# One b2 product for both experts of a tile: class-wise b2 rows and a third register a tile in a GNN + top-2 MoE kernel

## The chip, the cores and the metric

The kernel runs on one core of a Trainium2 chip. The metric is the device time of one execution in microseconds. Three executions of the kernel before took 361.08, 362.18 and 362.03 us, median 362.03.

## What is computed

```python
# x: (64 graphs, 128 nodes, 128), adj: (64, 128, 128), f32 / int32
def gnn(h, adj, W, a):                       # graph attention
    Wh = h @ W
    e = leaky_relu(s1[:, :, None] + s2[:, None, :], 0.2)    # s1, s2 = Wh @ a1, Wh @ a2
    attn = softmax(where(adj > 0, e, -9e15), axis=2)
    return attn @ Wh
def ffn(x, gate_w, gate_b, W1, b1, W2, b2):  # 8 experts, D = 128, H = 256, top 2
    probs = softmax(xf @ gate_w + gate_b)
    top2_vals, top2_idx = top_k(probs, 2)    # weights cw[token, expert], not renormalised
    for each expert e: acc += cw[:, e] * (gelu(xf @ W1[e] + b1[e]) @ W2[e] + b2[e])
x = x + gnn(layernorm(x), adj, W, a)
x = x + ffn(layernorm(x), ...)
```

There are 64 x 128 = 8192 tokens, and each goes through two of eight experts.

## The kernel before, in words

The program has two parts. The first works on groups of 8 graphs (8 groups): layer norm, attention, the first residual, and the router. The router gives every token an unordered pair of experts, one of NC = 28 classes, and a place in the region of its class; POOL scatters the rows of each graph to `sorted_rows` in HBM by these places. Part two runs over NT = 91 tiles of 128 rows, each of one class, so that a tile needs just two experts.

Which rows and which experts a tile has is known only at run time. It stands in a table, `tile_rows`, with three numbers a tile: its first row, its first expert, its second expert. DVE works it out in the last group in small steps (`early_1` to `early_10`; `of_tile` has one row for each of the three numbers), TensorE turns the columns into rows with one product for each number (`turn_table`, L1339), and ACT copies them into `tile_rows` (`copy_table`, L524), where every engine reads them. A second table, for the tiles from NE = 21 on, is made in the same way (`late_1` to `late_12`) between the first eleven tiles and turned at tile 11.

In the loop over tiles, SP loads the rows `xt` (with a register load for the first row), ACT normalises them into `xn` (L557), TensorE transposes (`turn`, L1354), ACT copies to `xnT` (L538), DVE copies W1 and b1 of the two experts to `pair_w` (L846, a register load for each expert), TensorE makes the four products upward (`up`, L1364), ACT applies gelu and writes `hid` (L548), TensorE makes the products downward (`down`, L1383 and L1385), DVE adds the two experts' results, weighted, to the residual (L1170, L1173), and POOL scatters the rows to `out`.

TensorE's order of one tile n is: load a register with the first expert (L1369); `turn(n + 2)`; `up(n + 1)`; load the second expert's register; `down(n)`. `down` has for each expert k one bf16 product that opens the accumulation, a stationary 65 x 128 of ones with b2's row as the moving operand (65 partitions, because b2 is split in three bf16 parts on partitions 0, 32 and 64), and two f32 products with W2. b2's parts lie in the last 128 columns of each expert's block in `experts`, as the upper halves of f32 words, and are therefore read with a step of 2. In program order the waits of `turn` (L1353), `up` (L1360) and `down` (L1378) stand between them as semaphore instructions.

b2's three parts are made by POOL at the start in eight steps, counted by `b2_step` (L357 to L372); TensorE waits for the eighth only at tile 0. After it POOL has nothing to do until the first rows are scattered at 69 us.

Of the kernel before, what the change touches and what calls it, by code (L numbers as in the profile page):

```python
# [7 lines left out]
BF16 = mybir.dt.bfloat16  # L8
I32 = mybir.dt.int32
ALU = mybir.AluOpType  # L10
ACT = mybir.ActivationFunctionType
AX_X = mybir.AxisListType.X

P = 128
GB = 8
E = 8
HC = 2
NC = E * (E - 1) // 2
# [7 lines left out]
SHIFT, RSTD, CWA, CWB, TOK = 128, 129, 130, 131, 132  # L26
B1 = HC * P
W2C = B1 + HC
B2C = W2C + HC * P
WCOLS = B2C + P  # L30
XR = 12
WR = 3
NO_TOKEN = 1 << 20
# [2 lines left out]
XB = 5  # L36
WB = 3
BOUNDED = "the table holds numbers of experts, 0 to 7"
EPS = 1e-5


def build(nc, x, adj, W, a, gate_w, gate_b, W1, b1, W2, b2, out, sorted_rows):
# [7 lines left out]
    with ExitStack() as ctx:  # L50
        def sb(name, shape, dt=F32):
            return ctx.enter_context(nc.sbuf_tensor(name, shape, dt))

        def sem(name):
            return ctx.enter_context(nc.semaphore(name))

        wh_ps = ctx.enter_context(nc.psum_tensor("wh_ps", [P, 3, 512], F32))
        at_ps = ctx.enter_context(nc.psum_tensor("at_ps", [P, 3, 512], F32))
# [6 lines left out]
        ones_bf = sb("ones_bf", [P, 512], BF16)  # L65
# [6 lines left out]
        class_no = sb("class_no", [P, NC])  # L72
# [3 lines left out]
        pair = sb("pair", [P, 2, NC])  # L76
# [14 lines left out]
        b2_raw = sb("b2_raw", [65, E, P])  # L91
        b2_part = sb("b2_part", [65, E, P], BF16)
        b2_rest = sb("b2_rest", [65, E, P])
        experts = sb("experts", [P, E, WCOLS])
        pair_w = sb("pair_w", [P, WR, 2, W2C])

# [41 lines left out]
        tiles_i = sb("tiles_i", [P, NC], I32)  # L138
        cum = sb("cum", [P, 2, NC])
        here = sb("here", [P, 3, NC])  # L140
        of_tile = sb("of_tile", [P, 3, NC])
        early_rows = sb("early_rows", [P, NC])
        clip = sb("clip", [P, 2, NC])
        tile_cols = sb("tile_cols", [P, 2, 3])
        tile_rows = sb("tile_rows", [1, 2, 3, P], I32)


        xt = sb("xt", [P, XR, ROW])
# [18 lines left out]
        b2_step = sem("b2_step")  # L167
# [35 lines left out]
        early_step = sem("early_step")  # L203
        table_step = sem("table_step")
# [91 lines left out]
        def _(pool):  # L296
# [30 lines left out]
            for hi in range(2, E + 1):  # L327
                at = (hi - 1) * (hi - 2) // 2
# [25 lines left out]
                rstd_of_start(g)  # L354


            nc.gpsimd.memset(experts[:, :, B2C:WCOLS], 0.0).then_inc(b2_step, 1)  # L357
            pool.wait_ge(b2_loaded, 48)
            pool.wait_ge(b2_step, 1)
            nc.gpsimd.tensor_copy(b2_part[:, :, :], b2_raw[:, :, :]).then_inc(b2_step, 1)  # L360
            pool.wait_ge(b2_step, 2)
            nc.gpsimd.tensor_copy(experts[0:1, :, B2C:WCOLS], b2_part[0:1, :, :]).then_inc(b2_step, 1)
            pool.wait_ge(b2_step, 3)
            nc.gpsimd.tensor_tensor(b2_rest[:, :, :], b2_raw[:, :, :], b2_part[:, :, :], ALU.subtract).then_inc(b2_step, 1)
            pool.wait_ge(b2_step, 4)
            nc.gpsimd.tensor_copy(b2_part[:, :, :], b2_rest[:, :, :]).then_inc(b2_step, 1)
            pool.wait_ge(b2_step, 5)
            nc.gpsimd.tensor_copy(experts[32:33, :, B2C:WCOLS], b2_part[32:33, :, :]).then_inc(b2_step, 1)
            pool.wait_ge(b2_step, 6)
            nc.gpsimd.tensor_tensor(b2_raw[:, :, :], b2_rest[:, :, :], b2_part[:, :, :], ALU.subtract).then_inc(b2_step, 1)  # L370
            pool.wait_ge(b2_step, 7)
            nc.gpsimd.tensor_copy(experts[64:65, :, B2C:WCOLS], b2_raw[64:65, :, :]).then_inc(b2_step, 1)  # L372
            pool.wait_ge(b2_step, 8)

            for g in range(NG - 1):
                pool.wait_ge(place_step, PL * (g + 1))
# [3 lines left out]
            last = (NG - 1) * GB  # L380
# [8 lines left out]
        def _(act):  # L389
# [131 lines left out]
            def copy_table(late):  # L521
                src = at_ps if late else wh_ps
                act.wait_ge(table_done, late + 1)
                nc.scalar.activation(tile_rows[0:1, late, :, :].rearrange("o k n -> o (k n)"), src[0:1, 2, 0:3 * P], ACT.Copy)\  # L524
                    .then_inc(table_ready, 1)

            copy_rank(NG - 2)
            copy_table(0)
            rough_rstd(NG - 1)
            exp_router(NG - 1)  # L530
# [43 lines left out]
        def _(dve):  # L574
            def stats_at_start(g):
# [4 lines left out]
                if g >= 1:  # L580
# [95 lines left out]
            def norms_2(i):  # L676
# [43 lines left out]
            m1, k1, total, p1, e2, p2, k2, df, qa, qb, hi, lo, tri, cls = (small[:, j, :] for j in range(14))  # L720
# [143 lines left out]
            def early_4():  # L864
                dve.wait_ge(early_step, 3)
                nc.vector.tensor_copy(cum[:, 0, :], tiles_i[:, :])
                nc.vector.tensor_copy(here[:, 2, :], tiles_i[:, :])
                nc.vector.tensor_scalar(part[:, :], part[:, :], float(P), None, ALU.mult)
                nc.vector.tensor_copy(of_tile[:, 1:3, :], pair[:, :, :]).then_inc(early_step, 1)

            def early_sum(k):
                step = 1 << k
# [21 lines left out]

            def early_8():
                dve.wait_ge(early_step, 12)
                nc.vector.tensor_tensor(of_tile[:, :, :], of_tile[:, :, :], here[:, None, 2, :].broadcast_to([P, 3, NC]),
                                        ALU.mult).then_inc(early_step, 1)

            def early_9():  # L900
# [218 lines left out]
            def late_5():  # L1119
                dve.wait_ge(table_step, 4)  # L1120
                nc.vector.tensor_copy(cum[:, 0, :], tiles_i[:, :])
                nc.vector.tensor_copy(here[:, 2, :], tiles_i[:, :])
                nc.vector.tensor_copy(of_tile[:, 1:3, :], pair[:, :, :]).then_inc(table_step, 1)

            def late_sum(k):
                step = 1 << k
# [18 lines left out]

            def late_9():
                dve.wait_ge(table_step, 13)
                nc.vector.tensor_tensor(of_tile[:, :, :], of_tile[:, :, :], here[:, None, 2, :].broadcast_to([P, 3, NC]),
                                        ALU.mult).then_inc(table_step, 1)

            def late_10():
# [53 lines left out]
        def _(pe):  # L1205
# [126 lines left out]
            def turn_table(late):  # L1332
                dst = at_ps if late else wh_ps
                if late:
                    pe.wait_ge(table_step, 17)
                else:
                    pe.wait_ge(early_step, 15)
                for k in range(3):
                    last = nc.tensor.matmul(dst[0:1, 2, k * P:(k + 1) * P], tile_cols[:, late, k:k + 1], ident[:, :],  # L1339
                                            start=True, stop=True)  # L1340
                last.then_inc(table_done, 1)
# [2 lines left out]
            turn_table(0)  # L1344
            keep_busy_later(16)
            count_ranks(NG - 1)

            experts_bf = experts[:, :, :].bitcast(BF16)

            def turn(n):  # L1350
                pe.wait_ge(xn_ready, n + 1)
# [16 lines left out]
            def load_expert(n, k):  # L1368
                return nc.values_load(entry(n, 1 + k), engines=[mybir.EngineType.PE], min_val=0, max_val=E - 1,  # L1369
                                      skip_runtime_bounds_check_because=BOUNDED)  # L1370

            def down(n, chosen_pair):
                pe.wait_ge(hid_ready, n + 1)
                if n == 0:
                    pe.wait_ge(b2_step, 8)
                    pe.wait_ge(experts_loaded, 48)
                if n >= 2:
                    pe.wait_ge(o_step, OS * (n - 1))  # L1378
                for k in range(2):
                    cols = slice(k * P, (k + 1) * P)  # L1380
                    e = chosen_pair[k]
                    b2_rows = experts_bf[0:65, bass.ds(e, 1), 2 * B2C + 1:2 * WCOLS:2]
                    nc.tensor.matmul(at_ps[:, n % 2, cols], ones_bf[0:65, 0:P], b2_rows, start=True, stop=False)  # L1383
                    for c in range(HC):
                        last = nc.tensor.matmul(at_ps[:, n % 2, cols], hid[:, n % WR, k * HC + c, :],  # L1385
                                                experts[:, bass.ds(e, 1), W2C + c * P:W2C + (c + 1) * P],
                                                start=False, stop=(c == HC - 1))
                last.then_inc(down_done, 1)

            pe.wait_ge(table_ready, 1)  # L1390
# [4 lines left out]
            for n in range(NT):  # L1395
                if n == 11:
                    turn_table(1)
                if n == NE:
                    pe.wait_ge(table_ready, 2)
                first = load_expert(n, 0)  # L1400
                if n + 2 < NT:
                    turn(n + 2)
                if n + 1 < NT:
                    up(n + 1)
                second = load_expert(n, 1)
                down(n, (first, second))


_INS = ["x", "adj", "L0_gnn_W", "L0_gnn_a", "L0_ffn_gate_w", "L0_ffn_gate_b", "L0_ffn_W1", "L0_ffn_b1", "L0_ffn_W2",
# [19 lines left out]
```

## Time and profile before

| | |
|---|---|
| median of three executions | 362.03 us |
| the profiled execution | 361.37 us, span 359.5 us |
| granted TensorE clock, mean | 0.919 |
| PE / weight load (PEld) busy | 310.7 us (86%) / 280.3 us (78%) |
| DVE / ACT / POOL busy | 244.4 us (68%) / 249.4 us (69%) / 178.8 us (50%) |
| DMA | 28.07 MB, mean 78 GB/s |
| chain that ended last, by engine | PE 60%, DVE 24%, ACT 5%, issue 4%, POOL 3% |
| chain, by line | PE L1385 24%, PE L1364 23%, DVE L637 4%, PE L1383 3%, PE L1354 3% |

PE is TensorE's matmuls, PEld its weight loads, which overlap them; ends of matmuls are modelled. Instructions that only the sequencer handles (register loads, register computations, semaphore instructions) aren't counted as busy; they appear under the engine's name with a q (PEldq for TensorE). The chain is followed back from the last instruction to what released each step. The part over the tiles runs from about 150 to 349 us, the part before it from 0 to 150.

### The profile page before, as it was taken

To read this page: it belongs to the slowest core of one execution; us is meant where nothing else is said; L and a number is where in the kernel's file an instruction comes from. 1 tells how busy PE (TensorE), PEld (TensorE's weight loads), DVE (VectorE), ACT (ScalarE), POOL (GpSimd) and SP (SyncE) were. 2 spreads that over 40 slices of the span, in tenths; PEclk is the share of its full clock that TensorE was granted. 3 is DMA by queue.
4 is the path that set the end of the run, shared out by engine and by line. 5 is a ranking of instruction groups with operands and counts; after the bars stand their busy time and mean duration, and the time that the engine had idled before them with its cause. 6 is when DMAs were issued, how large, how long until landed. Compare 5 with 4: busy or idle time off the path is not lost.

```text
span 359.5 us, 9425 instructions
## 1 busy us (share of the span) xinstructions
PE 310.7 (86%) x2390; PEld 280.3 (78%) x2390; DVE 244.4 (68%) x1056; ACT 249.4 (69%) x796; POOL 178.8 (50%) x203
## 2 busy tenths in 40 slices
PE   6878598988898608599999999999999999999960
PEld 3667387777677404399899999999999999999960
DVE  5664979999988996657755666656665666566630
ACT  3568477766765411388788888888888888888830
POOL 4939200266466677757634544454444444444450
PEclk9989878898878976789999999999999999999995
DMA  6990321429911111432222212222222112121000
GB/s 190 284 292 13 111 70 50 124 61 206 131 54 38 47 54 53 104 77 86 78 66 58 63 47 54 67 60 67 69 61 70 48 53 64 49 51 50 4 0 0
DMA packets 42231, 28.07 MB, mean 78 GB/s; under 512 B 5188, under 2 KB 40030, under 8 KB 42182
## 3 DMA queue, kind: packets, MB, share of 16 engines
q1 hardware_dynamic: 37222, 18.69, 22.2%
q0 software_dynamic: 4960, 8.80, 8.2%
q8 instruction: 22, 0.36, 0.4%
q14 instruction: 27, 0.22, 0.2%
HBM read 16.78 MB, written 12.23 MB: 81 GB/s over the span
## 4 chain that ended last, share of the span: by engine, by line
PE 60%; DVE 24%; ACT 5%; issue 4%; POOL 3%; DMA 1%; POOLq 0%; DVEq 0%; ACTq 0%
PE at_ps L1385 24%; PE wh_ps L1364 23%; DVE rows L637 4%; PE at_ps L1383 3%; PE q_ps L1354 3%; PE at_ps L1292 2%; ACT probs L442 2%; DVE bn L657 2%; DVE less_max L615 2%; DVE lrelu L610 2%; PE q_ps L1284 2%; DVE bn L665 1%; DMA xin<-in_x 1%; PE wh_ps L1251 1%; POOL rstd_start L299 1%
## 5 line engine op out<-in xcount | busy, mean ns | idle before, releaser
L348 POOL DMA_INDIRECT out_x<-o_sb,xt x91 | 89.7, 986 | 98.7 <-DVE o_sb L1173 91.6
L548 ACT ACTIVATE hid<-wh_ps,pair_w 128x128 f32<-128x128 f32 x364 | 104.1, 368 | 24.1 <-PE wh_ps L1364 23.9
L1385 PE MATMUL at_ps<-experts,hid 128*128 x728 | 110.8, 287 | 0.0
L1364 PE MATMUL wh_ps<-xnT,pair_w 128*128 128x128 f32 x728 | 98.3, 279 | 0.1
L1385 PEld LDWEIGHTS at_ps<-experts,hid 128*128 128x128 f32 x728 | 96.1, 192 | 2.2
L341 POOL DMA_INDIRECT sorted_rows<-rows,pos x64 | 62.5, 976 | 60.9 <-DVE pos L838 43.5
L1364 PEld LDWEIGHTS wh_ps<-xnT,pair_w 128*128 128x128 f32 x728 | 90.2, 195 | 0.6 <-issue 0.4
L846 DVE COPY pair_w<-experts 128x258 f32 x182 | 55.0, 302 | 29.2 <-issue 20.4
L1170 DVE SCALAR_TENSOR_TENSOR o_sb<-at_ps,xt 128x128 f32<-128x128 f32 x91 | 31.9, 350 | 45.9 <-PE at_ps L1385 45.5
L557 ACT ACTIVATE xn<-xt 128x128 f32<-128x128 f32 x91 | 43.9, 484 | 0.1
L1383 PE MATMUL at_ps<-experts,ones_bf 65*128 x182 | 40.9, 225 | 0.2 <-ACT hid L548 0.2
L1173 DVE SCALAR_TENSOR_TENSOR o_sb<-at_ps,xt,o_sb 128x128 f32<-128x128 f32 x91 | 31.9, 351 | 3.2
L538 ACT ACTIVATE xnT<-q_ps 128x128 f32<-128x128 f32 x91 | 25.2, 277 | 7.3 <-PE q_ps L1354 0.4
L1354 PE MATMUL q_ps<-ident,xn 128*128 128x128 f32 x91 | 25.2, 279 | 0.9 <-ACT xn L557 0.9
L442 ACT ACTIVATE probs<-lrelu,less_max 128x128 f32<-128x128 f32 x64 | 19.5, 387 | 7.9 <-DVE less_max L615 7.8
L1292 PE MATMUL at_ps<-wh,probsT 128*128 128x139 f32 x128 | 24.1, 359 | 0.2 <-ACT probsT L451 0.2
L1292 PEld LDWEIGHTS at_ps<-wh,probsT 128*128 128x128 f32 x128 | 22.4, 258 | 2.4 <-issue 1.8
L1284 PE MATMUL q_ps<-ident,probs 128*128 128x128 f32 x64 | 13.8, 383 | 11.9 <-ACT scores L433 8.7
L637 DVE SCALAR_TENSOR_TENSOR rows<-at_ps,rowinv,xin 128x128 f32<-128x128 f32 x64 | 21.6, 345 | 0.1
L1251 PE MATMUL wh_ps<-w_ext,xT 128*128 128x146 f32 x128 | 19.3, 307 | 2.7 <-ACT xT L401 2.7
L1284 PEld LDWEIGHTS q_ps<-ident,probs 128*128 128x128 f32 x64 | 10.8, 197 | 13.5 <-ACT probs L442 13.4
L1251 PEld LDWEIGHTS wh_ps<-w_ext,xT 128*128 128x128 f32 x128 | 17.7, 204 | 4.0 <-ACT x_gate L419 2.1
(200 smaller groups left out, 391.4 us busy)
## 6 DMA issues: line engine op xcount, KB each, us to landing
xt<-sorted_rows SPq DMA_DIRECT2D x91, 66.5 KB, 1.9
xin<-in_x SPq DMA_DIRECT2D x8, 512.0 KB, 5.4
adj_sb<-in_adj SPq DMA_DIRECT2D x8, 512.0 KB, 5.3
sorted_rows<-no_row SPq DMA_DIRECT2D x1, 1862.0 KB, 19.9
out_x<-o_sb,xt POOLq DMA_INDIRECT x91
experts<-in_L_ffn_W SPq DMA_DIRECT2D x1, 1024.0 KB, 9.3
experts<-in_L_ffn_W SPq DMA_DIRECT2D x2, 512.0 KB, 8.7
sorted_rows<-rows,pos POOLq DMA_INDIRECT x64, 2.5
```

Of the source, the lines that this page charges most:

```text
L341: nc.gpsimd.indirect_dma_start(out=sorted_rows, out_offset=bass.IndirectOffsetOnAxis(ap=pos[:, t:t + 1], axis=0), in_=rows[:, t, :], in_of ...
L348: nc.gpsimd.indirect_dma_start(out=out_v, out_offset=bass.IndirectOffsetOnAxis(ap=xt[:, n % XR, TOK:TOK + 1].bitcast(I32), axis=0), in_=o_ ...
L548: last = nc.scalar.activation(hid[:, n % WR, q, :], wh_ps[:, n % WR, q * P:(q + 1) * P], ACT.Gelu, bias=pair_w[:, n % WR, k, B1 + c:B1 + c ...
L557: nc.scalar.activation(xn[:, n % 2, :], t[:, 0:P], ACT.Identity, bias=t[:, SHIFT:SHIFT + 1], scale=t[:, RSTD:RSTD + 1]).then_inc(xn_ready, 1)
L637: last = nc.vector.scalar_tensor_tensor(out=rows[:, g * GB + k, 0:P], in0=src[:, o * (WK + 1):o * (WK + 1) + P], scalar=rowinv[:, k:k + 1] ...
L846: last = nc.vector.tensor_copy(pair_w[:, n % WR, k, :], experts[:, bass.ds(e, 1), 0:W2C])
L1251: last = nc.tensor.matmul(dst[:, o * WE:(o + 1) * WE], xT[:, k, :], w_ext[:, :], start=True, stop=True)
L1292: last = nc.tensor.matmul(dst[:, o * (WK + 1):(o + 1) * (WK + 1)], probsT[:, k, :], wh[:, g % WB, k, :], start=True, stop=True)
L1354: nc.tensor.transpose(q_ps[:, (n % 2) * 512:(n % 2) * 512 + P], xn[:, n % 2, :], ident[:, :]).then_inc(xnT_done, 1)
L1364: last = nc.tensor.matmul(wh_ps[:, n % WR, q * P:(q + 1) * P], pair_w[:, n % WR, k, c * P:(c + 1) * P], xnT[:, n % 2, :], start=True, stop ...
L1383: nc.tensor.matmul(at_ps[:, n % 2, cols], ones_bf[0:65, 0:P], b2_rows, start=True, stop=False)
L1385: last = nc.tensor.matmul(at_ps[:, n % 2, cols], hid[:, n % WR, k * HC + c, :], experts[:, bass.ds(e, 1), W2C + c * P:W2C + (c + 1) * P], ...
```

## The change

b2's bf16 parts no longer lie in `experts`. POOL writes them to `b2_split` (65 x 8 x 128, bf16) and then lays them side by side for each of the 28 classes in `b2_pairs` (65 x 28 x 256, bf16): for each first expert one copy that broadcasts its rows over all its classes, and for each class one copy of the second expert's rows, 7 + 28 copies. `down` opens both experts' accumulations with one product of 256 columns, chosen by the tile's class. So the table has a fourth number, the class, which TensorE loads into a register of its own (`load_class`) ahead of the first expert's.

```diff
-            nc.gpsimd.memset(experts[:, :, B2C:WCOLS], 0.0).then_inc(b2_step, 1)
+            nc.gpsimd.memset(b2_split[:, :, :], 0.0).then_inc(b2_step, 1)
...
-            nc.gpsimd.tensor_copy(experts[64:65, :, B2C:WCOLS], b2_raw[64:65, :, :]).then_inc(b2_step, 1)
+            nc.gpsimd.tensor_copy(b2_split[64:65, :, :], b2_raw[64:65, :, :]).then_inc(b2_step, 1)
             pool.wait_ge(b2_step, 8)
+            for hi in range(2, E + 1):
+                at = (hi - 1) * (hi - 2) // 2
+                nc.gpsimd.tensor_copy(b2_pairs[:, at:at + hi - 1, 0:P],
+                                      b2_split[:, E - hi:E - hi + 1, :].broadcast_to([65, hi - 1, P]))
+                for j in range(hi - 1):
+                    last = nc.gpsimd.tensor_copy(b2_pairs[:, at + j, P:2 * P], b2_split[:, E - 1 - j, :])
+            last.then_inc(b2_step, 1)
+            pool.wait_ge(b2_step, 9)
...
-                nc.scalar.activation(tile_rows[0:1, late, :, :].rearrange("o k n -> o (k n)"), src[0:1, 2, 0:3 * P], ACT.Copy)\
+                nc.scalar.activation(tile_rows[0:1, late, :, :].rearrange("o k n -> o (k n)"), src[0:1, 2, 0:4 * P], ACT.Copy)\
...
-                nc.vector.tensor_copy(of_tile[:, 1:3, :], pair[:, :, :]).then_inc(early_step, 1)
+                nc.vector.tensor_copy(of_tile[:, 1:3, :], pair[:, :, :])
+                nc.vector.tensor_copy(of_tile[:, 3, :], class_no[:, :]).then_inc(early_step, 1)
...
-                for k in range(3):
+                for k in range(4):
                     last = nc.tensor.matmul(dst[0:1, 2, k * P:(k + 1) * P], tile_cols[:, late, k:k + 1], ident[:, :],
...
+            def load_class(n):
+                return nc.values_load(entry(n, 3), engines=[mybir.EngineType.PE], min_val=0, max_val=NC - 1,
+                                      skip_runtime_bounds_check_because=CLASSES)
...
+                nc.tensor.matmul(at_ps[:, n % 2, 0:2 * P], ones_bf[0:65, 0:P], b2_pairs[:, bass.ds(of_class, 1), :],
+                                 start=True, stop=False)
                 for k in range(2):
                     cols = slice(k * P, (k + 1) * P)
                     e = chosen_pair[k]
-                    b2_rows = experts_bf[0:65, bass.ds(e, 1), 2 * B2C + 1:2 * WCOLS:2]
-                    nc.tensor.matmul(at_ps[:, n % 2, cols], ones_bf[0:65, 0:P], b2_rows, start=True, stop=False)
                     for c in range(HC):
...
-                                                start=False, stop=(c == HC - 1))
+                                                start=False, stop=(k == 1 and c == HC - 1))
...
+                of_class = load_class(n)
                 first = load_expert(n, 0)
                 if n + 2 < NT:
                     turn(n + 2)
                 if n + 1 < NT:
                     up(n + 1)
                 second = load_expert(n, 1)
-                down(n, (first, second))
+                down(n, of_class, (first, second))
```

The copies of parts 0 and 1 of b2 go to `b2_split` in the same way; `early_8` and `late_9` multiply four rows of 28 instead of three; `late_5` has the same additional copy of `class_no` as `early_4`. `WCOLS`, the width of an expert's block in `experts`, falls by 128.

## Rows read from the trace of the kernel before

**Rows 1.** Busy time and granted clock (PEclk) by stretch, all engines
```profile
core 0: us, PE busy (x) PEld busy (x) DVE busy (x) ACT busy (x) POOL busy (x), PEclk, DMA share, GB/s
240.00:280.00 40.00, 40.00 (x362) 39.55 (x360) 24.55 (x76) 34.08 (x114) 18.37 (x19) 1.00 0.24 66
```

**Rows 2.** Waits, 160 to 345 us: total, times, longest in us
```profile
DVE o_sb L1170 <- PE at_ps L1385: 39.0, 81, 1.7
ACT hid L548 <- PE wh_ps L1364: 21.0, 84, 0.6
PEld q_ps L1354 <- issue: 0.2, 1, 0.2
```

**Rows 3.** Transposes of line 1354: count, duration ns min/median/max, first and last start
```profile
L1354 PE MATMUL q_ps<-ident,xn x76: 272/273/273, 182.8 to 342.0; 128*128 128x128 f32 x76
```

**Rows 4.** Timeline of TensorE's matmuls, one tile: start us, length us, what
```profile
240.22 0.27 PE L1354 MATMUL q_ps<-ident,xn 128*128 128x128 f32 x1
...
241.22 0.23 PE L1383 MATMUL at_ps<-experts,ones_bf 65*128 x1
241.28 0.66 PE L1385 MATMUL at_ps<-experts,hid 128*128 x4
241.78 0.22 PE L1383 MATMUL at_ps<-experts,ones_bf 65*128 x1
...
242.34 0.27 PE L1354 MATMUL q_ps<-ident,xn 128*128 128x128 f32 x1
```

**Rows 5.** Sequencer instructions of lines 1369 and 1378, all tiles
```profile
L1369 PEldq TENSOR_LOAD <-tile_rows x182: 293/303/607, 150.9 to 345.5; - x182
L1378 PEldq EVENT_SEMAPHORE  x89: 51/51/51, 158.0 to 345.9; - x89
```

**Rows 6.** The same by line in one loop of the sequencer, 208.70 to 210.73 us
```profile
L1378 PEldq EVENT_SEMAPHORE  x2: 51/51/51, 208.7 to 210.6; - x2
L1383 PEldq FUSED_REGOPS  x2: 55/55/55, 208.8 to 209.2; - x2
L1385 PEldq FUSED_REGOPS  x4: 51/53/55, 209.0 to 209.5; - x4
L1369 PEldq TENSOR_LOAD <-tile_rows x2: 303/304/304, 209.6 to 210.2; - x2
L1353 PEldq EVENT_SEMAPHORE  x1: 51/51/51, 210.0 to 210.0; - x1
L1360 PEldq EVENT_SEMAPHORE  x1: 51/51/51, 210.1 to 210.1; - x1
L1383 PE MATMUL at_ps<-experts,ones_bf x2: 223/224/225, 209.3 to 209.9; 65*128 x2
```

**Rows 7.** Two successive starts of line 1378, in three other stretches
```profile
L1378 PEldq EVENT_SEMAPHORE  x2: 51/51/51, 206.2 to 208.7; - x2
L1378 PEldq EVENT_SEMAPHORE  x2: 51/51/51, 265.9 to 267.9; - x2
L1378 PEldq EVENT_SEMAPHORE  x2: 51/51/51, 270.2 to 272.1; - x2
```

**Rows 8.** Weight loads of bf16 products with 512 columns, 141 to 144 us
```profile
L1213 PEld LDWEIGHTS wh_ps<-ones_bf x12: 97/97/98, 141.2 to 143.6; 128*128 128x128 bf16 x12
```

**Rows 9.** Around the early table: timelines of PE and ACT, and a wait
```profile
138.59 1.44 PE L1339 MATMUL wh_ps<-ident,tile_cols 128*1 128x128 f32 x6
140.07 0.48 ACT L524 ACTIVATE tile_rows<-wh_ps 1x384 int32<-1x384 f32 x1 [0.99 <-PE wh_ps L1339]
DVE newton L699 <- ACT rough L459: 1.4, 1, 1.4
```

**Rows 10.** POOL's and DVE's timeline, 35 to 39 us, and line 610 throughout
```profile
35.11 2.15 POOL L370 TENSOR_TENSOR b_raw<-b_rest,b_part 65x1024 f32<-65x1024 f32 x1
37.32 1.38 POOL L372 COPY experts<-b_raw 1x1024 f32<-1x1024 f32 x1
35.19 4.05 DVE L610 SCALAR_TENSOR_TENSOR lrelu<-scores 128x512 f32<-128x512 f32 x2
L610 DVE SCALAR_TENSOR_TENSOR lrelu<-scores x16: 677/682/2615, 20.6 to 118.7; 128x512 f32<-128x512 f32 x16
```

More of the change, by code:

```diff
@@ L28 @@
 W2C = B1 + HC
-B2C = W2C + HC * P
-WCOLS = B2C + P
+WCOLS = W2C + HC * P
 XR = 12
@@ L38 @@
 BOUNDED = "the table holds numbers of experts, 0 to 7"
+CLASSES = "the table holds numbers of classes, 0 to 27"
 EPS = 1e-5
@@ L93, in build @@
         b2_rest = sb("b2_rest", [65, E, P])
+        b2_split = sb("b2_split", [65, E, P], BF16)
+        b2_pairs = sb("b2_pairs", [65, NC, 2 * P], BF16)
         experts = sb("experts", [P, E, WCOLS])
@@ L140, in build @@
         here = sb("here", [P, 3, NC])
-        of_tile = sb("of_tile", [P, 3, NC])
+        of_tile = sb("of_tile", [P, 4, NC])
         early_rows = sb("early_rows", [P, NC])
         clip = sb("clip", [P, 2, NC])
-        tile_cols = sb("tile_cols", [P, 2, 3])
-        tile_rows = sb("tile_rows", [1, 2, 3, P], I32)
+        tile_cols = sb("tile_cols", [P, 2, 4])
+        tile_rows = sb("tile_rows", [1, 2, 4, P], I32)
         xt = sb("xt", [P, XR, ROW])
@@ L361, in _ @@
             pool.wait_ge(b2_step, 2)
-            nc.gpsimd.tensor_copy(experts[0:1, :, B2C:WCOLS], b2_part[0:1, :, :]).then_inc(b2_step, 1)
+            nc.gpsimd.tensor_copy(b2_split[0:1, :, :], b2_part[0:1, :, :]).then_inc(b2_step, 1)
             pool.wait_ge(b2_step, 3)
@@ L367, in _ @@
             pool.wait_ge(b2_step, 5)
-            nc.gpsimd.tensor_copy(experts[32:33, :, B2C:WCOLS], b2_part[32:33, :, :]).then_inc(b2_step, 1)
+            nc.gpsimd.tensor_copy(b2_split[32:33, :, :], b2_part[32:33, :, :]).then_inc(b2_step, 1)
             pool.wait_ge(b2_step, 6)
@@ L896, in early_8 @@
                 dve.wait_ge(early_step, 12)
-                nc.vector.tensor_tensor(of_tile[:, :, :], of_tile[:, :, :], here[:, None, 2, :].broadcast_to([P, 3, NC]),
+                nc.vector.tensor_tensor(of_tile[:, :, :], of_tile[:, :, :], here[:, None, 2, :].broadcast_to([P, 4, NC]),
                                         ALU.mult).then_inc(early_step, 1)
@@ L1122, in late_5 @@
                 nc.vector.tensor_copy(here[:, 2, :], tiles_i[:, :])
-                nc.vector.tensor_copy(of_tile[:, 1:3, :], pair[:, :, :]).then_inc(table_step, 1)
+                nc.vector.tensor_copy(of_tile[:, 1:3, :], pair[:, :, :])
+                nc.vector.tensor_copy(of_tile[:, 3, :], class_no[:, :]).then_inc(table_step, 1)
             def late_sum(k):
@@ L1147, in late_9 @@
                 dve.wait_ge(table_step, 13)
-                nc.vector.tensor_tensor(of_tile[:, :, :], of_tile[:, :, :], here[:, None, 2, :].broadcast_to([P, 3, NC]),
+                nc.vector.tensor_tensor(of_tile[:, :, :], of_tile[:, :, :], here[:, None, 2, :].broadcast_to([P, 4, NC]),
                                         ALU.mult).then_inc(table_step, 1)
@@ L1346, in _ @@
             count_ranks(NG - 1)
-            experts_bf = experts[:, :, :].bitcast(BF16)
             def turn(n):
@@ L1370, in load_expert, with down @@
                                       skip_runtime_bounds_check_because=BOUNDED)
-            def down(n, chosen_pair):
+            def load_class(n):
+                return nc.values_load(entry(n, 3), engines=[mybir.EngineType.PE], min_val=0, max_val=NC - 1,
+                                      skip_runtime_bounds_check_because=CLASSES)
+            def down(n, of_class, chosen_pair):
                 pe.wait_ge(hid_ready, n + 1)
                 if n == 0:
-                    pe.wait_ge(b2_step, 8)
+                    pe.wait_ge(b2_step, 9)
                     pe.wait_ge(experts_loaded, 48)
```

## The prediction, made before the changed kernel had run

> **What bounds the kernel now.** I read the page's chain and the table by stretch first: from about 155 to 348 us the kernel runs one loop over 91 tiles, and in it TensorE is busy without a break, at a granted clock of 1.00, which is the 2.4 GHz level [rows 1]. The waits of the same stretch say who waits for whom: DVE and ACT wait for TensorE, and TensorE waits for nobody but once, 0.2 us [rows 2]. So the loop goes at the pace of TensorE. Its pace is very even: 76 tiles' transposes start between 182.8 and 342.0 us, 2.12 us apart [rows 3].
>
> What fills 2.12 us is seen in one tile [rows 4]. The profile shows each f32 product as two pairs of weight load and matmul, the transpose and each bf16 product as one. A tile has one pair for the transpose, 8 for the products up, 8 for the products down and 2 for b2's rows, 19 in all, and they follow each other 0.1115 us apart (2.118 / 19). The b2 product is no cheaper than the others although its 128 columns are done in 0.06 us: the matmul at 241.28 starts 0.06 us after the b2 matmul at 241.22, but the pairs (241.22 to 241.78 is five of them) still advance by 0.11, because the weights for the next pair are loaded meanwhile. A removed b2 product is therefore worth one whole step of 0.111 us to the array.
>
> The array is not the only thing with a pace. Its sequencer must also issue everything: per tile 38 loads and matmuls, 3 semaphore instructions, 6 register computations of 0.055 us for the run-time addresses and 2 register loads (TENSOR_LOAD) of 0.303 us [rows 5]. These are not counted as busy, so no share shows them; they must be laid out in time. Rows 6 do this for one loop in which nothing held the sequencer: semaphore at 208.7, register computations from 208.8 to 209.5, load at 209.6, semaphores at 210.0 and 210.1, load at 210.2, and the next tile's semaphore at 210.6. By these starts, a computation with its two or four array instructions takes 0.13 us (208.8 to 209.6 is six), and a register load with what follows it 0.36 (0.303, and the next instruction starts 0.05 later). The sum, 0.11 + 6 x 0.13 + 2 x 0.36 + 2 x 0.13, is 1.87 us; the loop of rows 6 took 1.9, and others that were not held took 1.9 and 2.0 [rows 7]. I take 1.95. The sequencer is thus only 0.17 us per tile (8%) faster than the array. It uses that to refill its lead after a stall: one loop took 2.5 us (206.2 to 208.7) and the next 1.9 [rows 7, 6]. This is the number on which the case turns.
>
> **The tile loop after the change.** For the array: one b2 product per tile less, and the one that stays has 256 columns. 512 columns of bf16 were loaded and multiplied 0.218 us apart (12 in a row) [rows 8], so 256 take 0.109, just as long as the load of the next weights beside it; the widened product fits in its step. 18 steps are 18 x 0.1115 = 2.007 us, 0.111 less than before. If the array still set the pace, 89 tiles would give 9.9 us back.
>
> For the sequencer: one register computation with its two array instructions goes (-0.13 us), and one register load comes (+0.36). It stands directly ahead of another register load, a pair that the trace doesn't show. Bounds: after a load the next instruction of the sequencer, even a semaphore instruction that doesn't use the value, starts 0.05 us after the load's end; by this a load costs 0.36. If the second load were sent while the first is under way, it would cost about as much as a semaphore instruction, 0.05 to 0.13. I take 0.36, because 0.31 + 0.05 is what every load in rows 6 shows, whatever follows it. The loop becomes 1.95 + 0.36 - 0.13 = 2.18 us. The rare longer loops (about 0.4 us more, as in rows 7; worked out from the starts of L1378, 89 from 158.0 to 345.9 [rows 5], of which four or five come that late) no longer have a spare 0.17 behind them that makes up for them: + 0.02. So 2.20 us a tile, set by the sequencer, against 2.12: + 0.075 us after rounding. For 88 tiles at this pace that is **+ 6.6 us**. The array then idles 0.19 us a tile, just before the transpose, since the two loads in a row stand ahead of it. Ends: the bare sum 1.87 + 0.23 = 2.10 gives - 1.8 us; 2.00 + 0.25 + 0.02 = 2.27 gives + 13 us.
>
> Two sentences of the Trainium skill speak on the price of a load. "DMA: Bandwidth & Descriptors", Latency and other measured facts, gives a floor of about 600 ns for a tensor_load; the median here is 303 ns and only the longest is 607 [rows 5], and by the page's figure the loop would be 2.5 us and the time some 30 us longer (an estimate from the page). "Advanced Engine Details and Errata", Sequencer Loop, says that engine instructions can be read and queued while the sequencer executes a control instruction. The trace bears that out for matmuls (none waits while a register is loaded), and shows nothing of a second load; carried over to it, it gives the first rival.
>
> Who else could be late: DVE waits 39.0 us in 81 tiles for TensorE and ACT 21.0 in 84 [rows 2], so at 2.0 us and more a tile both keep some slack, ACT least (0.25 us). The wait for hid stays hidden. The third entry needs no new DMA; the registers are TensorE's alone.
>
> **Ahead of the loop.** The table of tiles gets a fourth row. (a) The early table: one more product is two more pairs, and six took 1.44 us, the last of them running beyond the start of the next, so some 0.21 apart; ACT's copy waits for them, and behind it on ACT stand the logarithm and exponential that DVE's last routing chain waits for, 1.4 us [rows 9]. That is + 0.43. The copy grows from 384 to 512 elements, from its 0.48 us: + 0.12 (in proportion 0.16, less the fixed part). DVE's extra copy and wider product in the table add + 0.05 to 0.1 on the same chain. Together + 0.6. (b) The late table at tile 11 is two pairs more at the full clock, for which the array waits: + 0.2. (c) POOL. Today its f32 subtraction and copies (35.11 to 38.70) run beside DVE's products lrelu, and these took 4.05 us for two, where the median is 0.68 each [rows 10]. Whatever blocks them, DVE lost 2.7 us there. The new code has a smaller memset (bf16, 65 partitions) at the front, which moves the rest up to 0.5 us ahead of the collision: a gain of 0 to 0.5. Then it adds 35 copies of bf16 rows, 7168 elements at about 1 ns each by the copy of 1024 in 1.38 or less plus about 0.1 of fixed cost each: some 10 us, from 38.5 to 49. No one waits for them until tile 0 at 154, so as work they cost nothing. But DVE runs on: about fifteen of its small instructions from 43.5 to 49 read two operands; should each wait for half a copy (0.1 us), that is + 1.5. I take + 0.4 for (c) with ends - 0.5 and + 1.5, since most of DVE's time there goes into statistics, which read one operand, and into products from PSUM.
>
> "SBUF — State Buffer", its single rule on the shared port pair, calls this an exclusive lock between GpSimd and a DVE instruction with two SBUF inputs; the 4.05 us agree with it. By that rule the copies cost DVE something though the result is not needed for 100 us.
>
> **Sum.** The profiled execution took 361.4 us, 359.5 of them span; the median of the runs shown is 362.0, 0.7 above it. On the median: 362.0 + 6.6 + 0.6 + 0.2 + 0.4 = **369.8 us**. This case's own range is 360.5 to 377.
>
> **Rivals.** (1) The load is hidden. If a second load in a row costs under 0.19 us, the sequencer's loop stays below 2.007 and the array sets the pace: 362.0 - 9.9 + 1.2 = 353.3 us. For it: the sequencer is ahead of the array (in rows 6 the computation for the first b2 product stands at 208.8 and its matmul at 209.3), and two loads in a row are not in the trace. Against it: a queue covers a single stall, not a pace, and every load seen was waited out. (2) Between: a load costs 0.19 to 0.3, the period is 2.01 to 2.12, the gain in the loop is anything down to nothing and the 1.2 us ahead of it stay: 354 to 363, most likely near 360. This is also how it looks if much of the scatter between 1.87 and 1.95 is not inherent. (3) Loads in a row cost more than single ones, up to the 0.607 us of the longest one: 1.95 + 0.66 - 0.13 = 2.48, about 32 us more, 395. The forecast itself is the case on the other side from what the array's account alone says; the point from which it is slower is a load of 0.30 us (2.12 - 1.95 + 0.13), and loads are at 0.36.
>
> **Chances.** Forecast 0.75, rival 1 0.14, rival 2 0.09, rival 3 0.02. Range 360 to 375: it leaves out rival 1, rival 3 and the top tail. A measurement of this kernel can tell about 0.3% (1.1 us) from no change. Faster: 0.14 of rival 1, 0.05 of rival 2 and 0.02 of the forecast's lower end, 0.21; within 0.3%: 0.04 and 0.03, 0.07; slower 0.72.
>
> **What would show it.** Tiles of the new loop 2.15 to 2.25 us apart, with idle time of TensorE's weight loads before the transpose put down to issue, about 0.19 us a tile, where there is none now; three loads of 0.3 us a tile, 0.36 apart where two stand in a row; 18 pairs in a tile, with b2's matmul followed after 0.11 instead of 0.06; DVE and ACT waiting longer for TensorE. The step fails if the two loads start less than 0.2 us apart, or if the loop stays at 2.01 with no idle time. The part ahead fails if the first transpose of the loop (149.9) starts less than 0.3 or more than 2.5 us later.

## The result

| | before | after |
|---|---|---|
| median, five executions each | 362.03 us | 367.20 us |
| range | 361.08 to 363.19 | 366.40 to 367.58 |
| profiled span | 359.5 us | 365.6 us |

The ratio is 1.0153 (95% interval 1.0134 to 1.0173): the changed kernel is 5.5 us slower, 4.8 to 6.3 (the two medians are 5.2 apart; here and below, what a whole kernel gains or loses is worked out from its ratio). The head of its page:

```profile
span 365.6 us, 9288 instructions
PE 317.2 (87%) x2303; PEld 281.6 (77%) x2303; DVE 246.4 (67%) x1058; ACT 249.4 (68%) x796; POOL 190.3 (52%) x238
PE 60%; DVE 25%; ACT 4%; issue 3%; POOL 3%; DMA 1%; POOLq 0%; DVEq 0%; ACTq 0%
```

TensorE runs 87 pairs fewer and is busy longer. Where the 6.1 us of span came from is seen in two places. One is the positions of the scattered rows: the first of them are computed by DVE some 20 us behind POOL's copies, so what the copies cost DVE shows in their start. The next line gives their first and last start before and after (a count, ns min/median/max, first and last start). First the kernel before:

```profile
L838 DVE CAST pos<-pos_f x8: 146/152/347, 67.9 to 150.3; 128x8 int32<-128x8 f32 x8
```

and the changed kernel, with the transposes of the loop over tiles that answer to [rows 3]:

```profile
L850 DVE CAST pos<-pos_f x8: 147/154/233, 69.7 to 153.1; 128x8 int32<-128x8 f32 x8
L1366 PE MATMUL q_ps<-ident,xn x76: 299/300/303, 185.6 to 348.0; 128*128 128x128 f32 x76
```

So in this profile 1.8 us are lost ahead of 68 us, 1.0 more up to 182.8 us of the kernel before, and the rest behind it: 75 tiles there take (348.0 - 185.6) / 75 = 2.165 us each against 2.123 [rows 3], 0.042 more, together 3.2 us. The last part holds for these 75 tiles only. The fifteen intervals ahead of them, some of which hold waits for other engines, run from 149.9 to 182.8 us before and from 152.8 to 185.6 after: 32.9 us in both.

What the array and the sequencer did in one of these tiles is seen in three views of the changed kernel. The busy time by stretch, which answers to [rows 1] and has its columns:

```profile
240.00:280.00 40.00, 40.00 (x334) 38.54 (x334) 24.32 (x75) 33.18 (x111) 17.94 (x19) 1.00 0.23 64
```

TensorE's timeline, which answers to [rows 4]:

```profile
240.89 0.27 PE L1395 MATMUL at_ps<-b_pairs,ones_bf 65*128 x1
241.01 1.05 PE L1401 MATMUL at_ps<-experts,hid 128*128 x8
241.92 0.30 PE L1366 MATMUL q_ps<-ident,xn 128*128 128x128 f32 x1
242.05 1.12 PE L1376 MATMUL wh_ps<-xnT,pair_w 128*128 128x128 f32 x8
243.01 0.28 PE L1395 MATMUL at_ps<-b_pairs,ones_bf 65*128 x1
```

And the sequencer's instructions by line from 240.25 to 242.45 us, which answer to [rows 6]:

```profile
L1394 PEldq EVENT_SEMAPHORE  x2: 51/51/51, 240.3 to 242.4; - x2
L1395 PEldq FUSED_REGOPS  x1: 46/46/46, 240.4 to 240.4; - x1
L1401 PEldq FUSED_REGOPS  x4: 46/53/60, 240.5 to 240.9; - x4
L1385 PEldq TENSOR_LOAD <-tile_rows x1: 301/301/301, 241.1 to 241.1; - x1
L1381 PEldq TENSOR_LOAD <-tile_rows x2: 298/302/307, 241.4 to 242.1; - x2
L1365 PEldq EVENT_SEMAPHORE  x1: 51/51/51, 241.8 to 241.8; - x1
L1372 PEldq EVENT_SEMAPHORE  x1: 51/51/51, 241.9 to 241.9; - x1
```

The wide product is followed after 0.12 us and the 9 steps from 240.89 to 241.92 are 0.114 us long: it fits in its step. The two register loads in a row start 0.36 us apart (at 241.06 and 241.41, which the rows above round; third load 242.1). And the transpose, 241.92, starts at once behind the semaphore instruction of its wait (241.8): the array has caught up with its sequencer. A loop of the sequencer has no slack left anywhere; before, the second load stood in the median 0.29 us behind the semaphore instruction of `up` (L1360), 0.17 more than the 0.13 that it takes when nothing holds the sequencer; after the change the third load stands 0.13 us behind L1372 in the median. Note what the stretch says: PE is 40.00 us busy out of 40.00, as before, though 360 pairs would fit and 334 ran. Matmuls are drawn longer instead (the transpose 0.300 us against 0.273), so the busy share hides the sequencer's pace; the count and the distance of starts show it.

### The profile page after: what moved, and what is told of

The parts are those of the page before. It is cut to its first block, busy times and chain, and to the rows that moved or that the text cites. A ratio compares the mean times of both kernels' runs of the same rounds, so it can differ in the third digit from the quotient of the medians.

```text
span 365.6 us, 9288 instructions
## 1 busy us (share of the span) xinstructions
PE 317.2 (87%) x2303; PEld 281.6 (77%) x2303; DVE 246.4 (67%) x1058; ACT 249.4 (68%) x796; POOL 190.3 (52%) x238
## 4 chain that ended last, share of the span: by engine, by line
PE 60%; DVE 25%; ACT 4%; issue 3%; POOL 3%; DMA 1%; POOLq 0%; DVEq 0%; ACTq 0%
PE wh_ps L1376 24%; PE at_ps L1401 22%; PE q_ps L1366 5%; DVE rows L649 4%; PE at_ps L1395 3%; DVE bn L669 3%; DVE less_max L627 2%; PE at_ps L1306 2%; ACT probs L454 2%; DVE lrelu L622 2%; DVE bn L677 2%; PE q_ps L1298 2%; PE wh_ps L1265 1%; DMA xin<-in_x 1%; POOL rstd_start L301 1%
## 5 line engine op out<-in xcount | busy, mean ns | idle before, releaser
L1376 PE MATMUL wh_ps<-xnT,pair_w 128*128 128x128 f32 x728 | 103.1, 285 | 0.1
L1401 PE MATMUL at_ps<-experts,hid 128*128 x728 | 96.1, 275 | 0.0
L1401 PEld LDWEIGHTS at_ps<-experts,hid 128*128 128x128 f32 x728 | 88.6, 192 | 1.1
L1366 PE MATMUL q_ps<-ident,xn 128*128 128x128 f32 x91 | 27.6, 305 | 1.2 <-ACT xn L569 0.9
L1395 PE MATMUL at_ps<-b_pairs,ones_bf 65*128 x91 | 25.0, 275 | 0.4 <-ACT hid L560 0.4
```

The costliest lines, as they stand in the source:

```text
L1366: nc.tensor.transpose(q_ps[:, (n % 2) * 512:(n % 2) * 512 + P], xn[:, n % 2, :], ident[:, :]).then_inc(xnT_done, 1)
L1376: last = nc.tensor.matmul(wh_ps[:, n % WR, q * P:(q + 1) * P], pair_w[:, n % WR, k, c * P:(c + 1) * P], xnT[:, n % 2, :], start=True, stop ...
L1395: nc.tensor.matmul(at_ps[:, n % 2, 0:2 * P], ones_bf[0:65, 0:P], b2_pairs[:, bass.ds(of_class, 1), :], start=True, stop=False)
```

## The experiments

The theory: before, the array's 19 steps set the pace of the loop with 0.17 us to spare for the sequencer; the third register load makes the sequencer's loop longer than that, and the array's gain of 0.111 us is never seen. Rivals: the wide product or the shared accumulation costs the array something; two loads in a row are special; the whole loss lies ahead of the loop. Every ratio below is to the kernel before, run on the same chip beside it (medians 361.4 to 361.7).

**One load more, nothing else.**

```diff
+                third = load_expert(n, 0)
                 first = load_expert(n, 0)
...
-                    b2_rows = experts_bf[0:65, bass.ds(e, 1), 2 * B2C + 1:2 * WCOLS:2]
+                    b2_rows = experts_bf[0:65, bass.ds(e if k else third, 1), 2 * B2C + 1:2 * WCOLS:2]
```

> The kernel before, with one more register load a tile (the first expert once more, used for the address of the first b2 product) directly ahead of the present one; 19 steps of the array as before. Sequencer's pace: its loop of about 1.94 us becomes 2.30, against 2.12 now, so + 0.18 x 88 = + 16 us, 378. Rival, the array sets the pace and the load is covered: 362. Rival, two loads in a row overlap: 1.94 + 0.1 = 2.04, below 2.12, also 362.

378.78 us, ratio 1.0481 (1.0459 to 1.0504). Its transposes:

```profile
L1354 PE MATMUL q_ps<-ident,xn x76: 298/300/304, 185.2 to 358.7; 128*128 128x128 f32 x76
```

2.313 us a tile. With the array's work untouched, one load of 0.30 us a tile made the kernel 17.4 us slower. Both rivals in which the load is covered fall. With 0.36 us as the price of the load, the sequencer's loop before, without its waiting, comes to 2.313 - 0.36 = 1.95 us, scatter and rare long loops included.

**The changed kernel without its third load.**

```diff
-                of_class = load_class(n)
                 first = load_expert(n, 0)
...
-                down(n, of_class, (first, second))
+                down(n, first, (first, second))
```

> The changed kernel without the register load of the class: the wide product's row is picked by the first expert, so b2's part of the output is another one; all else stays. Sequencer's pace: the loop of the sequencer falls to about 1.81, the array's 18 steps of 0.1115 set the pace, 2.007; against the 2.166 measured after the change - 0.159 x 88 = - 14, so 353. Rival, the wide product or the shared accumulation costs the array what was lost: stays at 366 to 367.

354.07 us, ratio 0.9794 (0.9778 to 0.981).

```profile
L1366 PE MATMUL q_ps<-ident,xn x76: 272/273/273, 184.7 to 335.7; 128*128 128x128 f32 x76
```

2.013 us a tile, where 18 steps of 0.1115 are 2.007. The wide product still runs, but on the rows that the first expert's number picks, so b2's share of the output is another one; the work of the array is the same. The array does get the whole of its step back from the wide product, and the transposes are drawn with 0.273 us again. The rival of a costly wide product falls; one register load separates 354 from 367.

**The load away from the other one.**

```diff
-                of_class = load_class(n)
                 first = load_expert(n, 0)
                 if n + 2 < NT:
                     turn(n + 2)
+                of_class = load_class(n)
                 if n + 1 < NT:
                     up(n + 1)
```

> The changed kernel with the class's load moved behind the transpose, so that it no longer stands next to another load. Sequencer's pace: only the sum counts, 367.2 within 1 us. Rival, it is the two loads in a row, at the point where the sequencer's lead is smallest, that cost: the loop gets back part of 0.05 to 0.16 us a tile, 353 to 363.

366.45 us, ratio 1.0145 (1.0121 to 1.017), against 1.0153 (1.0134 to 1.0173) for the change; 2.161 us a tile against 2.165:

```profile
L1366 PE MATMUL q_ps<-ident,xn x76: 272/273/273, 184.7 to 346.8; 128*128 128x128 f32 x76
PEld wh_ps L1376 <- issue: 2.7, 13, 0.3
```

The place doesn't matter, as far as 1 us can be told; the sum does. What moves is where the array is short of work: the transposes are drawn with 0.273 us again, and the second line, from 200 to 330 us, shows waits for issue ahead of the products up in 13 of some 60 tiles, where the changed kernel shows none.

**POOL's part and the table's part, each alone.** The first makes b2_split and b2_pairs as the change does, keeps the loop and the table of before and reads b2 from b2_split; the second only adds the fourth row. What the first changes in the loop:

```diff
-                    b2_rows = experts_bf[0:65, bass.ds(e, 1), 2 * B2C + 1:2 * WCOLS:2]
-                    nc.tensor.matmul(at_ps[:, n % 2, cols], ones_bf[0:65, 0:P], b2_rows, start=True, stop=False)
+                    nc.tensor.matmul(at_ps[:, n % 2, cols], ones_bf[0:65, 0:P], b2_split[:, bass.ds(e, 1), :], start=True, stop=False)
```

> POOL's part of the change alone: b2_split and the 35 copies to b2_pairs are made, but the loop is the one before, with two b2 products of 128 columns (read from b2_split, so without a step of 2) and two register loads; the table has three rows. Theory: POOL's copies hold up DVE's small two-operand instructions, so the first scattered positions come 1.8 us later, as in the changed kernel, and nothing else changes: 361.4 + 1.8 = 363.2. Rival, the 1.8 us belongs to something else (loads from HBM, the profile's scatter): 361.4. Rival, reading b2 without the step of 2 speeds the loop: below 360.

363.02 us, ratio 1.0051 (1.0031 to 1.0071): + 1.8 us (1.1 to 2.6). The loop is as before (184.7 to 343.8 us for 75 tiles, 2.121 each), and the first positions come 2.4 us later in its profile:

```profile
L850 DVE CAST pos<-pos_f x8: 147/152/363, 70.3 to 152.4; 128x8 int32<-128x8 f32 x8
L1364 PE MATMUL q_ps<-ident,xn x76: 272/273/273, 184.7 to 343.8; 128*128 128x128 f32 x76
```

So reading without a step of 2 gives nothing in this loop, and POOL's part does cost. How is seen in the changed kernel's timelines of DVE and POOL:

```profile
44.09 2.04 DVE L684 TENSOR_TENSOR stat<-bn 128x16 f32<-128x16 f32 x1
46.06 0.29 DVE L685 TENSOR_TENSOR stat<-bn 128x8 f32<-128x8 f32 x1
```
```profile
44.01 1.23 POOL L383 COPY b_pairs<-b_split 65x128 bf16<-65x128 bf16 x5
45.19 0.82 POOL L380 COPY b_pairs<-b_split 65x768 bf16<-65x768 bf16 x1
45.96 0.81 POOL L383 COPY b_pairs<-b_split 65x128 bf16<-65x128 bf16 x3
```

L684 works on at most 16 elements a partition, takes 0.16 to 0.18 us at other times, and took 2.04 us while POOL's copies ran back to back. The Trainium skill, "SBUF — State Buffer", Who interferes with whom, has this as an exclusive lock between GpSimd and DVE; the trace agrees, and adds that this DVE instruction didn't get in between copies that followed each other without a gap: the five from 44.01 us and the broadcast of six rows from 45.19 all lie within its 2.04 us.

> The table's part of the change alone: four rows instead of three, the fourth unused; POOL and the loop as before. Theory: + 0.6 us for the early table (one product more at the lower clock, the larger copy on ACT), + 0.2 for the late one: 362.2. Rival, with the last rank products falling into a stretch of the lower clock, + 0.5 more: 362.7. Rival, hidden: 361.4.

362.13 us, ratio 1.0005 (0.9989 to 1.0021): + 0.2 us, not to be told from nothing (- 0.4 to + 0.8). Its profile shows two things that go against each other. The last rank products, ahead of the loop, come 0.6 us later and then run at the lower of the two clocks. First the kernel before, the products in the timeline and then the row by stretch around them (the granted clock is the third figure from the end); then the same two of the table's part alone:

```profile
147.43 0.60 PE L1305 MATMUL q_ps<-chosen,ones_bf 128*128 128x224 bf16 x8
```
```profile
147.30:149.00 1.70, 1.66 (x11) 0.94 (x11) 1.07 (x3) 0.00 (x0) 1.40 (x2) 0.71 0.40 111
```
```profile
148.07 1.05 PE L1307 MATMUL q_ps<-chosen,ones_bf 128*128 128x224 bf16 x8
```
```profile
147.80:150.00 2.20, 2.11 (x11) 1.45 (x11) 1.41 (x5) 0.00 (x0) 1.83 (x2) 0.50 0.57 139
```

That is about 0.5 us more, at 1.2 GHz throughout instead of in part. But at tile 11 the array then waits only 0.3 us for DVE's late table, where it waited 0.8 in the kernel before. The wait in the kernel before, and in the table's part alone:

```profile
PEld at_ps L1339 <- DVE tile_cols L1162: 0.8, 1, 0.8
```
```profile
PEld at_ps L1341 <- DVE tile_cols L1164: 0.3, 1, 0.3
```

**A gap behind each copy.** The changed kernel with a semaphore wait between any two of POOL's copies; the broadcasts of the first expert's rows get one in the same way.

```diff
-                    last = nc.gpsimd.tensor_copy(b2_pairs[:, at + j, P:2 * P], b2_split[:, E - 1 - j, :])
+                    nc.gpsimd.tensor_copy(b2_pairs[:, at + j, P:2 * P], b2_split[:, E - 1 - j, :]).then_inc(b2_step, 1)
+                    laid += 1
+                    pool.wait_ge(b2_step, laid)
```

> The changed kernel with a semaphore wait between any two of POOL's 35 copies, as the eight steps ahead of them have. Theory: in the changed kernel one DVE instruction of 0.16 us took 2.04 us while nine copies ran back to back; with a gap behind each copy DVE gets in after at most one, so 0.5 to 1.2 of the 1.8 us come back: 366.2. Rival, each copy delays one DVE instruction whatever the gap: 367.

366.80 us, ratio 1.0138 (1.0107 to 1.0169). The instruction in question is back to normal:

```profile
L687 DVE TENSOR_TENSOR stat<-bn x8: 153/178/187, 43.7 to 137.9; 128x16 f32<-128x16 f32 x4, 128x8 f32<-128x8 f32 x4
L853 DVE CAST pos<-pos_f x8: 146/152/366, 69.3 to 152.2; 128x8 int32<-128x8 f32 x8
```

The gap removes the long hold-up of L687 (longest 187 ns against 2044), but the positions still come 1.4 us later than in the kernel before (69.3 against 67.9), and the time isn't distinguishable from that of the change. Nor are the positions: the change and the kernel with POOL's part alone, whose POOL code is the same, have them at 69.7 and 70.3. DVE's delay of some 2 us at 44 us was mostly slack, for in the kernel before DVE waited just as long for TensorE a little later (the figure in brackets, in its timeline):

```profile
46.64 0.18 DVE L629 RECIPROCAL rowinv<-at_ps 128x3 f32<-128x3 f32 x1 [2.13 <-PE at_ps L1292]
```

Where the 1.4 us came from stands a little later in the same profile, in DVE's timeline and POOL's:

```profile
47.60 0.60 DVE L724 TENSOR_SCALAR newton<-newton 128x16 f32<-128x16 f32 x1
50.42 0.97 DVE L772 TENSOR_TENSOR logits<-logits,small 128x64 f32<-128x64 f32 x1
```
```profile
47.35 0.82 POOL L381 COPY b_pairs<-b_split 65x768 bf16<-65x768 bf16 x1
50.39 0.93 POOL L381 COPY b_pairs<-b_split 65x896 bf16<-65x896 bf16 x1
```

In the kernel before the same two DVE instructions took 0.16 and 0.21 us. Each ends within 0.1 us of the end of a broadcast of six or seven rows, so a single long copy holds DVE up by itself, gap or no gap, and the two make up 0.44 + 0.76 = 1.2 us. L724 reads a single tensor, so it doesn't take two operands to be held up. The changed kernel shows the same at 47.8 us, where DVE's first `newton` took 0.59 us beside the broadcast of seven rows. My expectation of 0.5 to 1.2 us was too high; the rival, a delay whatever the gap, is what happened with the long copies. Shorter broadcasts weren't tried.

**One register load instead of three.** If the sequencer is the bound, it is to be relieved, not the array. The table's fourth number holds everything: 64 x the place in b2_pairs + 8 x the first expert + the second.

```diff
-                of_class = load_class(n)
-                first = load_expert(n, 0)
+                word = load_class(n)
...
-                second = load_expert(n, 1)
-                down(n, of_class, (first, second))
+                down(n, nc.s_assert_within(word >> 6, 0, NC - 1, skip_runtime_bounds_check_because=CLASSES),
+                     ((word >> 3) & 7, word & 7))
```

Pairs lie in b2_pairs by ascending second expert, so that 7 copies do the work of 28. POOL makes the 28 numbers at the start.

> The changed kernel with one register load a tile instead of three on TensorE: the table's fourth number packs place in b2_pairs, first and second expert (64, 8, 1), and shifts and masks take it apart. POOL lays the pairs with 14 larger copies instead of 35. Sequencer's pace: 2.166 - 2 x 0.36 + at most 0.3 for the arithmetic = 1.75, so the array's 2.007 sets the pace: 353, about 1 less or more for POOL's copies ahead of the loop. Rival, register arithmetic costs as much as the loads: no gain over 367. Rival, the wide product costs the array: 366.

355.02 us, ratio 0.983 (0.9811 to 0.9849).

```profile
L1370 PE MATMUL q_ps<-ident,xn x76: 272/273/273, 184.1 to 335.6; 128*128 128x128 f32 x76
L1389 PEldq TENSOR_LOAD <-tile_rows x3: 298/300/307, 240.1 to 244.1; - x3
```

One load a tile (three in 240.0 to 244.4 us), 2.020 us a tile. The shifts and masks are three instructions of the sequencer a tile, six in the two tiles of the same stretch:

```profile
L1405 PEldq ALU_OP  x6: 32/36/36, 241.3 to 243.8; - x6
```

The next instruction starts 0.09 to 0.10 us behind each, so the three cost 0.3 us where two loads cost 0.72; the rival of the arithmetic falls. Nothing of the computation is left out, and it is 6.1 us faster than the kernel before.

**The same with POOL out of DVE's way.** The rows are laid by 14 transfers on SP's queue, behind the last load of adj.

```diff
+            sp.wait_ge(b2_step, 8)
+            for hi in range(2, E + 1):
+                at = (hi - 1) * (hi - 2) // 2
+                sp.dma_start(b2_pairs[:, at:at + hi - 1, 0:P],
+                             b2_split[:, E - hi:E - hi + 1, :].broadcast_to([65, hi - 1, P])).then_inc(b2_laid, 16)
+                sp.dma_start(b2_pairs[:, at:at + hi - 1, P:2 * P], b2_split[:, E - hi + 1:E, :]).then_inc(b2_laid, 16)
```

> As e6_one_word, but the rows are laid in b2_pairs by 14 transfers on SP's queue behind the last load of adj, not by POOL. Theory of the shared access of POOL and DVE: the 1.8 us ahead of the loop go away, 353.2 against 355.0. Rival, the transfers hold back the filling of sorted_rows behind them on the queue, or the 1.8 us have another cause: 355 or more.

353.83 us, ratio 0.9794 (0.9767 to 0.9821), the fastest of the kernels that leave nothing out. Its first positions start at 68.6 us, against 69.7 with POOL's copies and 67.9 before:

```profile
L855 DVE CAST pos<-pos_f x8: 148/153/366, 68.6 to 151.8; 128x8 int32<-128x8 f32 x8
```

The step from 0.983 is in the direction expected; the two intervals just overlap, so it isn't shown by the times alone. The 0.7 us of the first positions that remain have another cause, which the next run shows.

**Only the word.** The kernel before with one load a tile and its two b2 products (the table with four rows, b2 read from b2_split, no b2_pairs). Against the changed kernel, beside the edits for the word shown above:

```diff
-                nc.tensor.matmul(at_ps[:, n % 2, 0:2 * P], ones_bf[0:65, 0:P], b2_pairs[:, bass.ds(of_class, 1), :],
-                                 start=True, stop=False)
                 for k in range(2):
                     cols = slice(k * P, (k + 1) * P)
                     e = chosen_pair[k]
+                    nc.tensor.matmul(at_ps[:, n % 2, cols], ones_bf[0:65, 0:P], b2_split[:, bass.ds(e, 1), :], start=True, stop=False)
```

> The kernel before with only the packed word: one register load a tile on TensorE instead of two, but two b2 products of 128 columns as before (19 steps), no b2_pairs and none of its copies or transfers; the table has its fourth row. Theory: the array's 19 steps set the pace before and still do, 2.118 us a tile, so a lighter sequencer alone gives nothing: 361.6 to 362.5. Rival, the loads were already costing before: the loop under 2.10 and 359 or less.

362.94 us, ratio 1.0029 (1.0011 to 1.0047), and the loop at 2.120 us a tile:

```profile
L1363 PE MATMUL q_ps<-ident,xn x76: 272/273/273, 184.7 to 343.7; 128*128 128x128 f32 x76
```

A lighter sequencer alone gives nothing in the loop, as expected: before the change the array was the bound. The 1.0 us that it lost lies ahead of the loop and has its cause in the word. POOL makes the 28 packed numbers with eight more instructions at the start, and its `rstd_start`, for which DVE waits, comes 1.0 us later. First the kernel before, then this one:

```profile
15.92 1.67 POOL L299 TENSOR_TENSOR rstd_start<-stat_start,minus_half 128x8 f32<-128x8 f32 x1
```
```profile
16.92 1.67 POOL L303 TENSOR_TENSOR rstd_start<-stat_start,minus_half 128x8 f32<-128x8 f32 x1
```

The first positions follow by the same amount (68.9 against 67.9), though this kernel has none of the copies. In the two kernels with the word above, `rstd_start` starts at 16.75 (rows laid by POOL) and 16.64 us (by transfers), 0.8 and 0.7 later than before. So the 0.7 us left in the kernel with the transfers is this, and the copies cost the other one about 1 us, not 1.8.

Neither half of the idea pays alone: the word gives + 0.3%, the wide product with its third load + 1.5%. Together they give - 1.7%, and - 2.1% with the rows laid by transfers.

## Why the prediction was right, point by point

The forecast was 369.8 us in 360 to 375; 367.2 was measured. The direction and the mechanism of the loop held. Three sizes were off, and two of the errors worked against each other: the loop cost 3.4 us less than forecast, the part ahead of it 0.8 to 1.6 us more. That the total is only 2.6 us off is in part luck.

- **The array's side**: 0.111 us a tile from one b2 product less, the wide one within its step. Shown by the kernel without the third load, 2.013 us a tile.
- **The price of a load**: 0.36 us, in a row or apart. Shown in the sequencer's lines (241.1, 241.4) and by the load apart. The choice between 0.36 and 0.05 to 0.13, on which the case turned, was made because every load of [rows 6] was waited out by what stood behind it; that held for a second load too.
- **The loop's length** was put at 2.20 us and was 2.165. The term that was mis-sized is the removal of a b2 product: 2.313 - 2.165 = 0.148 us by the two kernels with three loads, where the smallest steps of [rows 6] had given 0.13. And the 0.02 for rare long loops was counted twice: 1.95 already holds them, as 2.313 - 0.36 shows. Together 0.035 us a tile. The number of tiles was off as well: the sum took 88 at this pace, while only the last 75 show it. The loop cost 3.2 us in the trace against + 6.6 forecast.
- **POOL**: put at + 0.4 with ends - 0.5 and + 1.5; alone it measured + 1.8 (1.1 to 2.6), above my upper end. The step that failed is the choice of + 0.4 instead of + 1.5, for the reason that "most of DVE's time there goes into statistics, which read one operand, and into products from PSUM": what counts is the small instructions in between, each of which can be held up for a whole copy, and one of those shown reads a single tensor. The smaller memset moved nothing ahead: it took 0.95 us in both kernels.
- **The table**: put at + 0.6 and + 0.2; measured + 0.2 (- 0.4 to + 0.8). In the profile the early part was + 0.6, and then two things came that weren't in the sum: the rank products at the lower clock, + 0.5, and a shorter wait at tile 11, - 0.5. That wait, 0.8 us before, lies in the stretch of [rows 2], where the forecast read that TensorE waits for nobody but once, 0.2 us; it overlooked it.
- The parts add up: 3.2 + 1.8 + 0.2 = 5.2 us against 5.5 (4.8 to 6.3).
- **Who else is late**: nobody, as said. DVE and ACT wait longer for TensorE than in [rows 2]:

```profile
DVE o_sb L1184 <- PE at_ps L1401: 43.9, 82, 1.7
ACT hid L560 <- PE wh_ps L1376: 27.1, 86, 0.7
```

- **What would show it**: two signs went against the forecast. The part ahead of the loop was to have failed if the first transpose started more than 2.5 us later than 149.9. It started at 152.8, 2.9 later, so by that sign the + 1.2 us ahead of the loop was wrong; POOL's part above is what it lacked. (Two other kernels with the same part ahead have it at 151.5 and 152.3, so one profile tells it to 1 us or so.) And one sign didn't appear. I expected 0.19 us a tile of idle weight loads, put down to issue. The shortage was drawn as longer matmuls instead (the transpose 0.300 us for 0.273), and PE stayed at 100%; the ends of matmuls are modelled.

Rival 1 (the load is hidden, 353.3 us) is what the kernel without the load did, 354.07; so its sum was sound and its condition false.

## What to carry to other kernels

An engine that is shown busy all the time can be close to another bound that no busy share counts, its own sequencer; here it was 8% away. Before taking work from such an engine, lay out one loop of register loads, register computations and semaphore instructions in time, look for the loop after a stall (there the sequencer runs free), and see what the new version adds to that sum. Here a register load of 0.30 us, 0.36 with its gap, cost more than three matmul steps; packing several run-time numbers in one word and taking them apart with shifts, 0.1 us each, is cheaper, and here paid only together with less work for the array.

## What the runs showed of the hardware that I had not expected

- Two register loads in a row didn't overlap: they start 0.36 us apart, as a load and a semaphore instruction do.
- A DVE instruction of 0.18 us took 2.04 us while POOL's bf16 copies of one to six rows ran without a gap; with a semaphore wait behind each copy its longest time was 0.187 us. Two other instructions of 0.16 and 0.21 us were then held up for 0.60 and 0.97 us, each by one copy of 0.82 and 0.93 us.
- In a loop paced by the sequencer the profile shows PE busy for 40.00 of 40.00 us, with 334 pairs where 362 had run.
